# Timing a GpSimd queue of indirect DMAs by ScalarE's probabilities instead of VectorE's maxima

## The chip, the cores and the metric

One NeuronCore of a Trainium2 chip runs the whole kernel. The metric is the device time of one execution in microseconds. The engines are TensorE (PE for matmuls, PEld for weight loads), VectorE (DVE), ScalarE (ACT), GpSimd (POOL) and SyncE (SP); each works through its own instructions in order, and they wait for one another on semaphores.

## The reference, cut to what matters

```python
# x: (B=2, L=2048, D=256); 16 heads of 16, so 32 (batch, head) pairs; TOP = L // 5 = 409
h = _layernorm(x) * (1 + ca) + sa
Q, K, V = proj(Wq, bq), proj(Wk, bk), proj(Wv, bv)            # each (32, 2048, 16)
_, top_idx = jax.lax.top_k(jnp.linalg.norm(Q, axis=2), 409)   # 409 queries per head
Q_sel = take_along_axis(Q, top_idx)
attn = softmax(Q_sel @ K.T * 0.25)                            # (32, 409, 2048)
out_full[top_idx] = attn @ V                                  # the other rows stay zero
x = x + ga * (out_full @ Wo.T + bo)
x = x + gb * moe(_layernorm(x) * (1 + cb) + sb)               # 8 experts, top 2
```

The change concerns the attention of the 409 selected queries over all 2048 keys, head by head. Here a "head" is one of the 32 (batch, head) pairs, counted n = 0 to 31.

## The kernel before, in words

The program is a sequence of blocks: setup, projection, selection of the top queries (`select_block`), attention (`attend_block`, from L797), routing and experts. Only `attend_block` is touched.

Within it, one head goes through five engines, and the work of neighbouring heads is interleaved:

- **SP** loads the keys of head n + 4 into one of four buffers (L869 to L876).
- **POOL** gathers the 409 selected query rows from DRAM by index: three indirect DMAs of 128 rows each (`gather_chunk`, L880 to L882) and, for four heads at once, one of the 25 last rows of each (`gather_tails`, L889). It copies a head's values into a padded layout (`spread_v`, L895). It writes the results back with indirect DMAs of the same kind: three per head (`scatter_chunk`, L899) and one for the tails of four heads (`scatter_tails`, L914).
- **PE** computes each head's scores twice. First as thirteen "chunks" a = 0 to 12 with the queries on partitions (`scores_chunk`, L1086, matmuls at L1094 and L1097), only so that the row maximum can be taken. Then as sixteen "tiles" j = 0 to 15 with the keys on partitions (`scores_tile`, L1101, matmul at L1110). The products with the values are `values` (L1113, matmul at L1120), four groups per head. `results` (L1124) adds up and turns the output; `turn_q` (L1059, L1065, L1069) transposes gathered queries; `turn_max` (L1132) transposes the maxima.
- **DVE** reduces each chunk to a maximum (`maximum`, L960, TENSOR_REDUCE at L963, semaphore `a_done`, thirteen per head), and normalises the results (`finish`, L979 to L988, semaphore `out_done`).
- **ACT** turns each tile into probabilities (`probability`, L1030, ACTIVATE at L1033, semaphore `prob_done`, sixteen per head). It also copies the transposed queries (L1024), the maxima (L1028) and the products (L1038).

The order on PE, ACT and DVE is written out by hand in their `run(n, u)`. In step n PE makes the tiles 0 to 15 of head n; beside tiles 1 to 7 the chunks 6 to 12 of head n + 1; beside tiles 9 to 14 the chunks 0 to 5 of head n + 2. `turn_q(n + 3)` stands at tile 8, `values(n, 0)` at tile 9, `values(n, 1)` at tile 11, `values(n, 2)` after tile 14, `values(n - 1, 3)` at tile 2 and `results(n - 1)` at tile 5. The heads 0 to 3 and 28 to 31 are written out straight; the heads 4 to 27 run in a hardware loop of four heads per trip (`steps`, L851), whose waits take their numbers from registers. POOL's program has no loop: L934 is a Python loop, so all its waits are for constants.

In step n POOL does up to nine things in this order: gathers of head n + 4 (chunks 0, 1, 2), `spread_v(n + 3)`, scatters of head n - 1 (chunks 0, 1, 2), and in every fourth step one tail scatter and one tail gather. Before each of the gathers, each of the scatters and the tails it calls `turn(n, at)` with `at` = 0 to 6, and this waits until another engine has come to a given place. In the kernel before that engine is DVE: `a_done` has to reach 13 (n + 1) + 7, 9, 11, 13, 15, 17, 19. In step n, counted in chunks, this is after the maxima of chunks 6, 8, 10 and 12 of head n + 1 and of chunks 1, 3 and 5 of head n + 2. The `min` in `turn` keeps the number within what DVE ever reaches: in step 31 all seven waits are for the last maximum of all.

Of the kernel before, what the change touches and what calls it, by code (L numbers as in the profile page):

```python
# [29 lines left out]
N = B * H  # L30
TPB = L // P
# [29 lines left out]
def wait(eng, sem, value):  # L61

    if isinstance(value, int) and value <= 0:
        return
    eng.wait_ge(sem, value)
# [731 lines left out]
def attend_block(nc, ctx, io, cst):  # L797

    with ExitStack() as own:
# [4 lines left out]
        NA = FULL * NK + 1  # L804
# [28 lines left out]
        a_ps, a_done, mrow_ps, mrow_done = sem("a_ps"), sem("a_done"), sem("mrow_ps"), sem("mrow_done")  # L833
        b_ps, prob_done, pv_ps, pvs_done, out_ps, out_done = sem("b_ps"), sem("prob_done"), sem("pv_ps"), sem("pvs_done"), sem("out_ps"), sem("out_done")
# [26 lines left out]
        def has(n):  # L861

            return not isinstance(n, int) or 0 <= n < N

        with nc.Block() as block:

            @block.sync
            def _(sp):
                def load_k(n, u):  # L869

                    wait(sp, b_ps, TPB * (n - U + 1))
                    rows = io["k3_d"][bass.ds(n, 1)].rearrange("a r d l -> (a r d) l")
                    for at, count in STACK_K:
                        sp.dma_start(kt[u][at * HD:(at + count) * HD, :], rows[0:count * HD, :]).then_inc(k_here[u], 16)

                steps(sp, load_k)  # L876

            @block.gpsimd
            def _(pool):
                def gather_chunk(n, c):  # L880
                    pool.indirect_dma_start(out=qsel[n % U][:, c, :], out_offset=None, in_=io["q3_d"],  # L881
                                            in_offset=bass.IndirectOffsetOnAxis(ap=cst["idx"][:, n, c:c + 1], axis=0)).then_inc(q_here[n % U], 16)  # L882

                def gather(n):
                    wait(pool, q_ps, n - U + 1)
                    for c in range(FULL):
                        gather_chunk(n, c)

                def gather_tails(g):  # L889

                    wait(pool, q_ps, GH * g)
                    pool.indirect_dma_start(out=qtail[:, :], out_offset=None, in_=io["q3_d"],
                                            in_offset=bass.IndirectOffsetOnAxis(ap=cst["tidx"][:, g:g + 1], axis=0)).then_inc(tail_here, 16)

                def spread_v(n):  # L895
                    wait(pool, pv_ps, GRP * (n - U + 1))
                    pool.tensor_copy(vh[n % U][:, :, 0:HD], vn[:, :, n, :]).then_inc(vh_done, 1)

                def scatter_chunk(n, c):  # L899
                    pool.indirect_dma_start(out=io["attn_d"], out_offset=bass.IndirectOffsetOnAxis(ap=cst["idx"][:, n, c:c + 1], axis=0),  # L900
                                            in_=outs[n % 2][:, c, :], in_offset=None).then_inc(scattered[n % 2], 16)

                def scatter(n):
                    pool.wait_ge(out_done, n + 1)
                    for c in range(FULL):
                        scatter_chunk(n, c)

                TURNS = (7, 9, 11, 13, 15, 17, 19)

                def turn(n, at):  # L910

                    wait(pool, a_done, min(NA * (n + 1) + TURNS[at], NA * N))

                def scatter_tails(g):  # L914

                    pool.wait_ge(out_done, GH * (g + 1))
                    pool.indirect_dma_start(out=io["attn_d"], out_offset=bass.IndirectOffsetOnAxis(ap=cst["tidx"][:, g:g + 1], axis=0),
                                            in_=otail[:, g, :], in_offset=None).then_inc(tail_out, 16)

                gather_tails(0)  # L920
                for n in range(3):
                    gather(n)
                step = Chain(pool, g_step)
                step(pool.memset(fold[:, :], 0.0))
                for g in range(GRP):
                    last = pool.affine_select(out=fold[:, :], in_=fold[:, :], compare_op=ALU.not_equal, fill=1.0,
                                              base=-32 * g, pattern=[[-1, HD + 1]], channel_multiplier=1)
                    if g < GRP - 1:
                        step(last)
                last.then_inc(fold_done, 1)  # L930
                for n in range(3):
                    spread_v(n)
                gather(3)
                for n in range(N):  # L934
                    if has(n + 4):
                        pool.wait_ge(q_ps, n + 1)
                        for c in range(FULL):
                            turn(n, c)
                            gather_chunk(n + 4, c)
                    if has(n + 3):  # L940
                        spread_v(n + 3)
                    if has(n - 1):
                        pool.wait_ge(out_done, n)
                        for c in range(FULL):
                            turn(n, FULL + c)
                            scatter_chunk(n - 1, c)
                    turn(n, 2 * FULL)
                    if n % GH == 1 and n > 1:
                        scatter_tails(n // GH - 1)
                    if n % GH == 0 and n // GH + 1 < GN:  # L950
                        gather_tails(n // GH + 1)
                scatter(N - 1)
                scatter_tails(GN - 1)
                for u in range(2):
                    pool.wait_ge(scattered[u], 16 * FULL * N // 2)
                pool.wait_ge(tail_out, 16 * GN)
# [933 lines left out]
```

## Time and profile before

| | us |
|---|---|
| median of 3 runs | 1300.29 |
| lowest and highest | 1293.09, 1305.63 |
| the profiled execution | 1293.09 |
| its span, first to last instruction | 1291.3 |

The profiled execution is the lowest of the three. In a row of the timeline, the first two numbers are the start and the length in us from the start of the span; `x2` means that so many instructions in a row were merged; in square brackets stand the idle time of the engine just before the row and what ended it.

### The profile page before, as it was taken

How to read it: one execution, taken by the hardware profiler on the slowest of the kernel's cores; microseconds unless marked ns; L12 is line 12 of the kernel's file. 1: busy time of each engine (PE TensorE's matmuls, PEld its weight loads, DVE VectorE, ACT ScalarE, POOL GpSimd, SP SyncE). 2: the span in 40 equal slices, each digit the busy share in tenths (PEclk: the TensorE clock that was granted, in tenths of full speed). 3: DMA queues.
4: the chain of work that ended last, by engine and by line, in shares of the span. 5: the costliest groups of instructions: out<-in, count | busy, mean ns of one | idle time of the engine just before them, and what ended most of it. 6: DMA issues, size and time to landing. Idle time of an engine off the chain costs nothing. (4 is left out here: it accounts for less than half of the span.)

```text
span 1291.3 us, 29412 instructions
## 1 busy us (share of the span) xinstructions
PE 1041.9 (81%) x7670; PEld 644.4 (50%) x7671; DVE 928.4 (72%) x2313; ACT 638.0 (49%) x1387; POOL 637.2 (49%) x660
## 2 busy tenths in 40 slices
PE   7997102699999999999947744599999999999991
PEld 4443002133333333333335631488888888888881
DVE  4884788787777777768438869477777777777771
ACT  2776274276676766667724520244444444444440
POOL 1787380455555455544258950244455444444541
PEclk9999555599999999989969965799999999999996
DMA  6344860111111111111049920122333222222325
GB/s 212 115 155 153 263 209 25 33 44 37 40 43 31 42 32 43 30 43 29 4 143 274 286 89 1 34 39 45 49 49 48 46 44 45 45 49 49 48 35 146
DMA packets 84388, 101.56 MB, mean 79 GB/s; under 512 B 17008, under 2 KB 71984, under 8 KB 84208
## 3 DMA queue, kind: packets, MB, share of 16 engines
q1 hardware_dynamic: 60792, 74.31, 19.0%
q0 software_dynamic: 21632, 23.11, 11.1%
q10 hardware_dynamic: 1912, 3.54, 0.8%
q8 instruction: 22, 0.36, 0.1%
q14 instruction: 30, 0.25, 0.1%
HBM read 62.26 MB, written 42.84 MB: 81 GB/s over the span
## 5 line engine op out<-in xcount | busy, mean ns | idle before, releaser
L963 DVE TENSOR_REDUCE attend_mxh<-attend_p_a 128x1 f32<-128x512 f32 x416 | 265.4, 686 | 83.8 <-PE attend_p_a L1094 64.6
L1033 ACT ACTIVATE w<-attend_p_b 128x409 f32<-128x409 f32 x480 | 227.4, 515 | 119.8 <-PE attend_p_b L1110 92.4
L1755 ACT ACTIVATE expert_hr<-expert_p,b1t 128x256 f32<-128x256 f32 x312 | 131.0, 471 | 223.3 <-PE expert_p L1706 219.7
L1667 POOL DMA_INDIRECT acc_d<-expert_ys,expert_drop x78 | 126.8, 1626 | 209.9 <-DVE expert_ys L1788 182.3
L1720 PE MATMUL expert_p<-w,expert_hhi 128*128 x1248 | 213.7, 273 | 5.8 <-DVE expert_hlo L1813 4.9
L1706 PE MATMUL expert_p<-expert_xhi,w 128*128 128x256 f16 x1248 | 214.3, 274 | 3.6 <-DVE expert_xlo L1796 1.5
L1720 PE MATMUL expert_p<-w,expert_hlo 128*128 x624 | 170.1, 273 | 0.0
L1110 PE MATMUL attend_p_b<-attend_qt,w 98*128 98x409 bf16 x480 | 164.9, 347 | 1.5 <-issue 1.2
L1094 PE MATMUL attend_p_a<-w,attend_qt 96*128 96x512 bf16 x384 | 151.8, 399 | 8.8 <-ACT attend_qt L1024 6.4
L900 POOL DMA_INDIRECT attn_d<-attend_outs,idx x96 | 93.9, 978 | 114.0 <-DVE attend_mxh L963 99.0
L1720 PEld LDWEIGHTS expert_p<-w,expert_hhi 128*128 128x128 f16 x1248 | 121.8, 98 | 28.7 <-issue 11.6
L881 POOL DMA_INDIRECT attend_qsel<-q_d,idx x96 | 92.2, 960 | 88.4 <-DVE attend_mxh L963 69.5
L1706 PEld LDWEIGHTS expert_p<-expert_xhi,w 128*128 x1248 | 122.7, 98 | 23.3 <-issue 8.4
L1659 POOL DMA_INDIRECT expert_xs<-h_d,expert_take x78 | 86.5, 1109 | 84.1 <-DVE expert_take L1792 61.2
L1120 PE MATMUL attend_p_o<-w,attend_vh 128*32 128x409 f32 x1024 | 116.3, 526 | 5.8 <-issue 2.8
L1706 PE MATMUL expert_p<-expert_xlo,w 128*128 128x256 f16 x624 | 119.9, 274 | 0.0
L1811 DVE CAST expert_hhi<-expert_hr 128x512 f16<-128x512 f32 x156 | 67.8, 435 | 65.9 <-ACT expert_hr L1755 64.5
L1813 DVE TENSOR_TENSOR expert_hlo<-expert_hr,expert_hhi 128x512 f16<-128x512 f32 x156 | 109.1, 700 | 5.4
L1110 PEld LDWEIGHTS attend_p_b<-attend_qt,w 98*128 98x128 bf16 x480 | 46.4, 98 | 116.4 <-ACT w L1033 77.1
L1706 PEld LDWEIGHTS expert_p<-expert_xlo,w 128*128 x624 | 61.4, 98 | 7.2
L1720 PEld LDWEIGHTS expert_p<-w,expert_hlo 128*128 128x128 f16 x624 | 61.1, 98 | 6.2
L1747 ACT ACTIVATE expert_xhi<-expert_p_x 128x512 f16<-128x512 f32 x39 | 23.3, 597 | 79.6 <-PE expert_p_x L1692 79.6
(303 smaller groups left out, 1694.6 us busy)
## 6 DMA issues: line engine op xcount, KB each, us to landing
q_d<-project_q SPq DMA_DIRECT2D x32, 256.0 KB
w<-in_L_ffn_w SPq DMA_DIRECT2D x16, 512.0 KB, 3.9
route_wraw<-in_L_ffn_w SPq DMA_DIRECT2D x16, 512.0 KB, 4.9
w<-k_d SPq DMA_DIRECT2D x32, 192.0 KB
k_d<-project_k SPq DMA_DIRECT2D x45, 128.0 KB
x<-in_L_attn_x SPq DMA_DIRECT2D x8, 512.0 KB, 11.2
attn_d<-zero SPq DMA_DIRECT2D x8, 512.0 KB
w<-k_d SPq DMA_DIRECT2D x32, 128.0 KB
```

Of the source, the lines that this page charges most:

```text
L881: pool.indirect_dma_start(out=qsel[n % U][:, c, :], out_offset=None, in_=io["q3_d"], in_offset=bass.IndirectOffsetOnAxis(ap=cst["idx"][:, ...
L900: pool.indirect_dma_start(out=io["attn_d"], out_offset=bass.IndirectOffsetOnAxis(ap=cst["idx"][:, n, c:c + 1], axis=0), in_=outs[n % 2][:, ...
L963: dve.tensor_reduce(mxh[:, c, k:k + 1], chunk_bank(a)[:, :], AX, ALU.max).then_inc(a_done, 1)
L1033: act.activation(prob[:, j, :], tile_bank(j)[:, 0:TOP], ACT.Exp, scale=SCALE).then_inc(prob_done, 1)
L1094: last = pe.matmul(into[:, :], qt[u][0:KR, c * P:(c + 1) * P], kt[u][0:KR, k * CH:(k + 1) * CH], start=True, stop=True)
L1110: pe.matmul(tile_bank(j)[:, 0:TOP], kt[u][0:KR + 2, j * P:(j + 1) * P], qt[u][0:KR + 2, 0:TOP], start=True, stop=True).then_inc(b_ps, 1)
L1120: last = pe.matmul(p_o[32 * w:32 * w + VC, 0:TOP], vh[u][:, j, :], prob[:, j, :], start=(g == 0), stop=(g == TPB // GRP - 1), tile_positio ...
L1667: pool.indirect_dma_start(out=io["acc_d"], out_offset=bass.IndirectOffsetOnAxis(ap=drop[u][:, s:s + 1], axis=0), in_=ys[u][:, s, :], in_of ...
L1706: last = pe.matmul(p_1[g][:, f, :], w, xp[u][:, k, :], start=(n == 0), stop=(n == 3 * KD - 1))
L1720: last = pe.matmul(p_2[s][:, 0:D], hp[u][:, f, s * P:(s + 1) * P], w, start=(f == 0 and n == 0), stop=(f == FB - 1 and n == 2))
L1755: act.activation(hr[g % 2][:, f, :], p_1[g][:, f, :], ACT.Relu, bias=cst["b1t"][:, bass.ds(e * FB + 2 * g + f, 1)], scale=1.0 / WSCALE).th ...
L1813: dve.tensor_tensor(hlo[u][:, 2 * g:2 * g + 2, :], hr[g % 2][:, :, :], hhi[u][:, 2 * g:2 * g + 2, :], ALU.subtract).then_inc(hlo_done, 1)
```

## The change

One table and one wait of the POOL program. The seven turns wait for ACT's probabilities of step n's own head, `prob_done`, sixteen per head, in place of DVE's maxima. The value for turn 0 is 16 n, that is, all tiles of head n - 1; for n = 0 it is zero and `wait` leaves it out. The others are reached after tiles 2, 4, 7, 10, 12 and 14 of head n. Nothing is added or taken away, on any engine; each operation's order on its queue stays.

```diff
-                TURNS = (7, 9, 11, 13, 15, 17, 19)
+                TURNS = (0, 3, 5, 8, 11, 13, 15)
 
                 def turn(n, at):
 
-                    wait(pool, a_done, min(NA * (n + 1) + TURNS[at], NA * N))
+                    wait(pool, prob_done, TPB * n + TURNS[at])
```

The waits beside them stay: `gather` for `q_ps`, `spread_v` for `pv_ps`, the scatters for `out_done`.

## Rows read from the trace of the kernel before

**Rows 1.** Busy time by stage. Columns as in the header line.
```profile
core 0: us, PE busy (x) PEld busy (x) DVE busy (x) ACT busy (x) POOL busy (x), PEclk, DMA share, GB/s
261.27:296.23 34.96, 34.96 (x266) 12.82 (x265) 28.87 (x66) 25.96 (x59) 19.11 (x22) 1.00 0.17 42
296.23:601.97 305.74, 290.86 (x2115) 103.82 (x2112) 232.99 (x528) 205.86 (x458) 161.38 (x180) 0.98 0.15 38
601.97:634.96 32.99, 32.53 (x234) 11.58 (x232) 25.04 (x60) 24.91 (x55) 10.02 (x11) 1.00 0.05 15
```

**Rows 2.** Waits of POOL, 296 to 590 us.
```profile
POOL attn_d L900 <- DVE attend_mxh L963: 67.7, 63, 2.5
POOL attend_qsel L881 <- DVE attend_mxh L963: 51.0, 30, 4.4
```

**Rows 3.** Timeline of ACT: tile 0 (from bank p_a) and tiles 14, 15, straight heads.
```profile
272.90 0.51 ACT L1033 ACTIVATE w<-attend_p_a 128x409 f32<-128x409 f32 x1
...
283.06 0.51 ACT L1033 ACTIVATE w<-attend_p_b 128x409 f32<-128x409 f32 x1
284.12 0.51 ACT L1033 ACTIVATE w<-attend_p_b 128x409 f32<-128x409 f32 x1 [0.55 <-issue]
284.53 0.51 ACT L1033 ACTIVATE w<-attend_p_a 128x409 f32<-128x409 f32 x1
```

**Rows 4.** Timeline of ACT: head 4 and its neighbours.
```profile
296.23 0.51 ACT L1033 ACTIVATE w<-attend_p_a 128x409 f32<-128x409 f32 x1
...
302.19 0.92 ACT L1033 ACTIVATE w<-attend_p_b 128x409 f32<-128x409 f32 x2 [1.06 <-PE attend_p_b L1110]
...
306.66 0.51 ACT L1033 ACTIVATE w<-attend_p_b 128x409 f32<-128x409 f32 x1
308.37 0.51 ACT L1033 ACTIVATE w<-attend_p_b 128x409 f32<-128x409 f32 x1 [1.20 <-PE attend_p_b L1110]
308.78 0.51 ACT L1033 ACTIVATE w<-attend_p_a 128x409 f32<-128x409 f32 x1
```

**Rows 5.** Timeline of POOL: head 4's step.
```profile
297.82 0.99 POOL L881 DMA_INDIRECT attend_qsel<-q_d,idx  x1 [2.27 <-DVE attend_mxh L963]
299.11 0.96 POOL L881 DMA_INDIRECT attend_qsel<-q_d,idx  x1 [0.30 <-issue]
300.38 0.95 POOL L881 DMA_INDIRECT attend_qsel<-q_d,idx  x1 [0.30 <-issue]
301.34 0.41 POOL L897 COPY attend_vh<-v 128x256 f32<-128x256 f32 x1
303.58 1.01 POOL L900 DMA_INDIRECT attn_d<-attend_outs,idx  x1 [1.84 <-DVE attend_mxh L963]
305.56 0.97 POOL L900 DMA_INDIRECT attn_d<-attend_outs,idx  x1 [0.98 <-DVE attend_mxh L963]
306.84 0.96 POOL L900 DMA_INDIRECT attn_d<-attend_outs,idx  x1 [0.30 <-DVE attend_mxh L963]
308.11 0.99 POOL L892 DMA_INDIRECT attend_qtail<-q_d,tidx  x1 [0.30 <-issue]
```

**Rows 6.** Timeline of PE: tile 15 of head 4 and what precedes it.
```profile
306.52 0.90 PE L1120 MATMUL attend_p_o<-w,attend_vh 128*32 128x409 f32 x8
307.34 0.35 PE L1110 MATMUL attend_p_b<-attend_qt,w 98*128 98x409 bf16 x1
```

**Rows 7.** Timeline of DVE: the two maxima before head 4's first gather.
```profile
296.32 1.29 DVE L963 TENSOR_REDUCE attend_mxh<-attend_p_a 128x1 f32<-128x512 f32 x2 [0.90 <-PE attend_p_a L1094]
```

**Rows 8.** Timeline of ACT: head 8.
```profile
346.11 0.51 ACT L1033 ACTIVATE w<-attend_p_a 128x409 f32<-128x409 f32 x1
...
350.71 0.51 ACT L1033 ACTIVATE w<-attend_p_b 128x409 f32<-128x409 f32 x1 [1.65 <-issue]
...
358.66 0.51 ACT L1033 ACTIVATE w<-attend_p_a 128x409 f32<-128x409 f32 x1
```

**Rows 9.** Timeline of POOL: first gather and tail gather of step 8, first gather of step 9.
```profile
347.16 0.98 POOL L881 DMA_INDIRECT attend_qsel<-q_d,idx  x1 [2.22 <-DVE attend_mxh L963]
...
358.01 0.99 POOL L892 DMA_INDIRECT attend_qtail<-q_d,tidx  x1 [0.30 <-issue]
359.83 0.96 POOL L881 DMA_INDIRECT attend_qsel<-q_d,idx  x1 [0.83 <-DVE attend_mxh L963]
```

**Rows 10.** Timeline of ACT: tile 3 of head 9, tile 0 of head 10.
```profile
361.29 0.51 ACT L1033 ACTIVATE w<-attend_p_b 128x409 f32<-128x409 f32 x1 [1.31 <-PE attend_p_b L1110]
...
372.10 0.51 ACT L1033 ACTIVATE w<-attend_p_a 128x409 f32<-128x409 f32 x1 [0.32 <-PE attend_p_b L1110]
```

**Rows 11.** Instructions of two lines: count, then shortest/median/longest in ns.
```profile
L963 DVE TENSOR_REDUCE attend_mxh<-attend_p_a x416: 669/681/693, 235.2 to 630.0; 128x1 f32<-128x512 f32 x139
...
L900 POOL DMA_INDIRECT attn_d<-attend_outs,idx x96: 956/972/1017, 268.0 to 650.3; - x96
```

**Rows 12.** Timeline of POOL: third scatter of step 2, a straight head.
```profile
282.96 0.96 POOL L900 DMA_INDIRECT attn_d<-attend_outs,idx  x1 [0.30 <-DVE attend_mxh L963]
```

**Rows 13.** Timeline of POOL: the end of the block.
```profile
642.52 0.96 POOL L900 DMA_INDIRECT attn_d<-attend_outs,idx  x1 [0.64 <-issue]
647.81 0.96 POOL L900 DMA_INDIRECT attn_d<-attend_outs,idx  x1 [4.33 <-DVE attend_otail L987]
```

## The prediction

> **What bounds the kernel now.** I read the busy times by stage first, then who waits for whom, then the timelines of POOL, ACT and PE side by side for single heads.
>
> The stage that the change touches runs from about 249 to 645 us. The stretches by stage [rows 1] part it in three: heads 1 to 3 (straight), heads 4 to 27 (loop), heads 28 to 30 (straight). In the first PE is busy 34.96 of 34.96 us, 11.65 us a head. In the loop it is busy 290.86 of 305.74 us: 12.74 us a head, 12.12 of them busy. DVE has 232.99, ACT 205.86, POOL 161.38, that is 53% for POOL. So PE sets the pace, in a ring with ACT and DVE, whose results free PE's banks. POOL is not short of time: the waits of POOL [rows 2] show 67.7 + 51.0 us in which it stood in a turn behind a DVE maximum.
>
> So POOL's turns cost nothing directly. What can be had or lost is the difference between a loop head and a straight one, 12.74 - 11.65 = 1.09 us, over 24 heads 26.1 us, 2.0% of the whole. Where is it? Tile 0 of each head marks its start on ACT. A straight head takes 284.53 - 272.90 = 11.63 us, and its tiles 14 and 15 start 1.06 us apart [rows 3]. Head 4 takes 308.78 - 296.23 = 12.55; its tiles 14 and 15 stand 308.37 - 306.66 = 1.71 apart, and ACT had been idle 1.20 us behind PE; it had also been idle 1.06 us before tile 8 [rows 4]. Yet PE's row of tile 15 begins at 307.34 and takes 0.35 [rows 6]: it was finished, by that record, 0.68 us before ACT got it. In that time POOL's third scatter ran, 306.84 to 307.80 [rows 5]. The late tile 8 (302.19) likewise comes after the gathers and the copy, which ended at 301.75 [rows 5]. I read this as PE's completions coming late beside POOL's indirect DMAs. It is an inference from coincidence: in the straight head a third scatter at 282.96 stands just as close to tile 14 (283.06) and delays nothing [rows 3, 12].
>
> **The change part by part.** Nothing is added, so the sum is made of places. How far does each POOL operation move?
>
> - From the maximum to its gather: the maximum of chunk 6 ends at 296.32 + 0.69 = 297.01, the gather starts at 297.82 [rows 5, 7], 0.81 later. A POOL operation behind another follows it by 0.30 [rows 5].
> - Turn 0 now waits for tile 15 of the head before. In head 4's frame that is 0.41 before tile 0 (308.37 against 308.78 [rows 4]) plus 0.51 for the tile: it ends at 0.10. With the 0.81 the first gather starts at 0.9, where it is now at 297.82 - 296.23 = 1.59. It comes 0.7 us earlier.
> - Turns 1 and 2 (tiles 2 and 4) are then met about when POOL is free; the gathers follow at some 2.2 and 3.5, the copy ends near 4.8, now at 5.52: 0.7 earlier.
> - The scatters wait for `out_done` (finish, unchanged) and tiles 7, 10 and 12. They come at roughly 6.5, 7.8 and 9.6, now at 7.35, 9.33 and 10.61 [rows 5]: 0.9 to 1.5 earlier. The tails wait for tile 14 (306.66 - 296.23 = 10.43, plus 0.51) and come near 11.2, now 11.88.
>
> What each is worth:
>
> 1. *Third scatter.* At 9.6 to 10.6 it is over before `values(n, 2)` (306.52, that is 10.29 [rows 6]) is half done. If the scatter is what holds tile 15, the heads without tails (two in four, 12 of the loop) get 1.71 - 1.06 = 0.65 us each: -7.8 us. In the other 12 the tails now stand where the scatter stood, and I count nothing. From below the gain is zero, since in the straight head the coincidence costs nothing.
> 2. *Gathers.* Tile 8 could come earlier, but I count zero. Head 8 is the trial: its first gather starts 347.16 - 346.11 = 1.05 after tile 0, 0.54 earlier than in head 4 [rows 8, 9]. The stall did not go; it moved to tile 6, 1.65 us [rows 8]. The head takes 358.66 - 346.11 = 12.55 us, exactly as head 4. What is cover here is the ring through `results`, `finish` and `values(n, 0)`, which ends at the same place either way.
> 3. *First gather against `values(n - 1, 3)`.* Both are now released by the same event, the end of tile 15. Head 9 shows the bad case: tails of the step before at 358.01, first gather at 359.83, 1.17 after its tile 0 [rows 8, 9], and tile 3 is late by an idle time of 1.31 us; the head takes 372.10 - 358.66 = 13.44 [rows 10], 0.89 more than head 4. Three loop heads (9, 21, 25; the rows are of 9) show it, all directly behind a tail gather. After the change two heads in four stand behind tails with a gather at 0.9. I charge the 9 of these 12 that do not have it now: 9 x 0.89 = +8.0 us. Bounds: 0 (head 8's gather at 1.05 delayed no tile 3) and 21 heads x 0.89 = +18.7.
>
> Free things: step 0 loses its first wait, so one gather is issued earlier, in a prologue where no turn follows it. Steps 30 and 31 are now paced, where most of their waits used to be for the last maximum; their scatters end by 643.48, and the next operation starts at 647.81, behind `out_done`, with 4.33 us idle before it [rows 13]. That is the cover; a delay over 4 us would be needed to reach the end. The key loads on SP wait for `b_ps` and are passed by nothing.
>
> Sum: -7.8 + 0 + 8.0 = +0.2 us. On the profiled execution's own 1293.09 that gives 1293.3. This execution is 0.55% below the median of the runs, so on the scale of the median the forecast is 1300.29 + 0.2, about 1300.
>
> A rule bears on term 3 and on the whole. The maxima's durations are 669 to 693 ns over 416 instructions, and the scatters' 956 to 1017, wherever the two meet [rows 11]: neither slows the other. The Trainium skill (SBUF — State Buffer, on which operations share GpSimd's port) says the same: `tensor_reduce` on trn2 never contends with GpSimd, and a DMA does not contend with a compute engine. By that rule alone the place of an indirect DMA is free, and the sum would be 0, 1300 us; by the late tiles, it is the difference of two terms of 8 us.
>
> **The rivals.**
>
> *Unchanged, the forecast* (chance 0.48): the stalls move and the ring gives the same period, as between heads 4 and 8; about 1300.
>
> *Faster* (0.25): with POOL 0.7 to 1.5 us earlier, gathers, scatters and PE's odd groups no longer meet. For: PE is busy without a gap in the straight heads; 0.65 us per head hang at tile 15. Against: head 8. All of it would be 26.1 us, 1274; half of it, 1287. It decides from 13 us on, 0.54 us a loop head.
>
> *Slower* (0.27): one mechanism, term 3 everywhere. The first gather at 0.9 always starts within `values(n - 1, 3)`, which needs the same tile 15, and tile 3 waits for the gather. 21 heads x 0.89 = 18.7 without the gain of term 1: 1319. Over the four straight heads with a gather too it is 25 x 0.89 = 22.3, 1322. It counts as slower from 15 heads on (15 x 0.89 = 13.3). For: heads 9, 21, 25. Against: head 8, whose gather at 1.05 does nothing to tile 3 [rows 8, 9].
>
> *The turns do nothing at all*, because POOL would be held by `out_done` and its own backlog: then again 1300; it is inside the first case. The idle times of POOL [rows 2] speak against it: it does stand in the turns.
>
> **How the numbers follow.** Likeliest is the unchanged time, 1300. The range leaves out one in ten at either side: below it goes to most of the faster case, 1278; above to the slower one's, 1320. Faster by over 1% (below 1287) takes nearly all of the faster case, slower by over 1% the slower one, and the rest falls within 1%: 0.24, 0.27 and 0.49. 1% is about what a measurement of this kernel tells from no change.
>
> **What would show it.** On POOL's timeline the first gather of a loop step should stand about 0.9 us after tile 0, the third scatter near 9.6, and its releaser should be ACT's L1033. If term 1 holds, tiles 14 and 15 stand 1.06 apart in heads without tails. If term 3 holds, tile 3 has over a microsecond of idle time before it and the tile-to-tile period is near 13.4. If a loop head takes about 12.5 with the stall at tile 6, term 2 is right. I am wrong if the loop falls below 12.2 or rises above 13.3 us a head, or if anything outside 249 to 645 us moves by more than a microsecond or two.

## The result and the profile after

The changed kernel takes 1315.58 us at the median of 13 runs (1309.08 to 1323.44), the kernel before 1305.63 at the median of 13 (1293.09 to 1310.72). The ratio is 1.0083, with a 95% interval of 1.0061 to 1.0105: slower by 0.8%, a little but outside the uncertainty of the measurement.

The profiled execution of the changed kernel took 1324.97 us (span 1323.2), more than any of its 13 timed runs, and the one of before (1293.09) was the fastest of its. The traces therefore show 31.9 us where the medians show 10. I read the kind of the loss from them, not its size, which is about three times too large; the second profile of the same kernel, in the experiments, is nearer to the medians.

Busy time by stage of the changed kernel; the stretches are the same pieces of work as the first two in [rows 1], cut where tile 0 of heads 1, 4 and 28 starts on ACT: the straight heads 1 to 3, and the 24 heads of the loop.

```profile
core 0: us, PE busy (x) PEld busy (x) DVE busy (x) ACT busy (x) POOL busy (x), PEclk, DMA share, GB/s
266.06:300.95 34.89, 34.89 (x266) 12.76 (x265) 28.88 (x66) 25.56 (x58) 18.92 (x22) 1.00 0.18 42
300.95:633.74 332.79, 313.14 (x2114) 107.43 (x2113) 236.28 (x528) 205.22 (x457) 160.81 (x180) 0.90 0.14 35
```

The straight heads 1 to 3 take 34.89 us, before 34.96. The loop takes 332.79 us, before 305.74: 13.87 us a head against 12.74, +27.05 us. Head 0 takes 3.4 us more and starts 1.4 us later, which with -0.1 us for heads 1 to 3 makes the 4.7 us by which the loop starts later. Behind the loop the two are alike (1323.2 - 633.74 = 689.5 us, before 1291.3 - 601.97 = 689.3). So 27.05 of the 31.9 us lie in the loop. The number of interest is PEclk: 0.98 in the loop before, 0.90 now. TensorE stands at one of two levels, 1.0 (2.4 GHz) or 0.5 (1.2 GHz), so the mean of 0.90 is 2 x 0.10 x 332.79 = 67 us at the lower one, before 2 x 0.02 x 305.74 = 12 us. The granted clock's own record has 68.3 and 10.2.

POOL's timeline in a loop head, head 7, whose tile 0 starts at 343.53:

```profile
344.44 0.98 POOL L881 DMA_INDIRECT attend_qsel<-q_d,idx  x1 [2.14 <-ACT w L1033]
345.73 0.96 POOL L881 DMA_INDIRECT attend_qsel<-q_d,idx  x1 [0.30 <-issue]
346.99 0.94 POOL L881 DMA_INDIRECT attend_qsel<-q_d,idx  x1 [0.30 <-issue]
347.94 0.40 POOL L897 COPY attend_vh<-v 128x256 f32<-128x256 f32 x1
350.51 1.01 POOL L900 DMA_INDIRECT attn_d<-attend_outs,idx  x1 [2.17 <-ACT w L1033]
352.13 0.97 POOL L900 DMA_INDIRECT attn_d<-attend_outs,idx  x1 [0.61 <-ACT w L1033]
353.93 0.96 POOL L900 DMA_INDIRECT attn_d<-attend_outs,idx  x1 [0.83 <-ACT w L1033]
```

The gathers start 0.91, 2.20 and 3.46 us after tile 0 and the copy ends at 4.81, as forecast (0.9, 2.2, 3.5, 4.8). The first gather and the scatters are released by ACT's L1033. The scatters come at 6.98, 8.60 and 10.40, half a microsecond or more later than forecast (6.5, 7.8, 9.6), because the tiles that release them are late. ACT in the same head:

```profile
343.53 0.51 ACT L1033 ACTIVATE w<-attend_p_a 128x409 f32<-128x409 f32 x1
...
345.99 0.92 ACT L1033 ACTIVATE w<-attend_p_b 128x409 f32<-128x409 f32 x2
348.80 1.72 ACT L1033 ACTIVATE w<-attend_p_b 128x409 f32<-128x409 f32 x4 [1.89 <-PE attend_p_b L1110]
...
354.88 0.51 ACT L1033 ACTIVATE w<-attend_p_b 128x409 f32<-128x409 f32 x1
355.95 0.51 ACT L1033 ACTIVATE w<-attend_p_b 128x409 f32<-128x409 f32 x1 [0.56 <-PE attend_p_b L1110]
356.49 0.51 ACT L1033 ACTIVATE w<-attend_p_a 128x409 f32<-128x409 f32 x1
```

Tiles 14 and 15 are 1.07 us apart, as in a straight head; in head 4 of before it was 1.71 [rows 4]. Tile 15, preceded by over a microsecond of idle time in 14 of the 24 loop heads before, is so in one now (head 16). In its place tile 6 is late (348.80, idle time 1.89), by over a microsecond in 20 of 24 heads; before it was in 4. PE and DVE at that place:

```profile
346.15 1.00 PE L1129 MATMUL attend_p_o<-attend_fold,attend_pvs 128*128 128x17 f32 x8
347.08 0.35 PE L1110 MATMUL attend_p_b<-attend_qt,w 98*128 98x409 bf16 x1
...
349.36 0.35 PE L1110 MATMUL attend_p_b<-attend_qt,w 98*128 98x409 bf16 x1 [0.53 <-ACT w L1033]
```
```profile
348.83 0.69 DVE L963 TENSOR_REDUCE attend_mxh<-attend_p_a 128x1 f32<-128x512 f32 x1 [1.54 <-PE attend_p_a L1097]
```

By its record PE has tile 6 (347.08) done at 347.43; ACT starts on it 1.37 us later. DVE takes up its next chunk at about the same moment, 348.83. The third gather's issue ended at 347.93. Over the 20 heads ACT takes up the late tile 6 between 0.48 and 0.98 us behind the end of that issue (15 of them 0.83 to 0.98) and never ahead of it. PE itself then stands for 0.53 us, for a bank that ACT has not freed. In the straight heads 1 to 3 of the same trace the third gather stands at the same place, 3.35 to 3.46 us after tile 0, and tile 6 is not late.

What this does to TensorE's clock is seen two heads on. Head 9 starts at 368.96, has the same late tile at 374.27 (ACT idle for 1.94 us), and takes up PE's work again at 374.84:

```profile
368.96:382.94 13.98, 13.28 (x90) 4.52 (x89) 9.91 (x22) 8.52 (x21) 7.12 (x9) 0.88 0.15 35
375.30:378.70 3.40, 3.28 (x13) 0.66 (x12) 3.06 (x11) 1.87 (x5) 1.26 (x2) 0.50 0.01 2
351.87:355.27 3.40, 3.37 (x27) 0.99 (x26) 3.24 (x8) 2.23 (x5) 1.93 (x2) 1.00 0.04 10
```

These are three stretches of the view by stage: head 9; 3.40 us in it from 375.30; and a stretch of equal length at the same place of head 7. In the second PE is at the lower level and starts 13 matmuls where it starts 27 in the third. Tiles 10 and 12 of head 9 are late for that. There are 20 such stretches of 3.4 us in the loop, three before.

The account of the loop's +27.05 us, from the starts of tile 0 and the granted clock of each head:

| loop heads | before | after |
|---|---|---|
| never at the lower level | 22, mean 12.55 us | 9, mean 12.63 us |
| one stretch at it | 1, 14.08 us | 10, mean 13.92 us |
| two | 1, 15.51 us | 5, mean 15.99 us |

With 12.63 as the base, the ten heads cost 10 x 1.29 = 12.9 us, the five 5 x 3.36 = 16.8, together 29.7; the two before cost 4.5 over 12.55; and 24 x 0.08 = 1.9 is left between the bases. 29.7 - 4.5 + 1.9 = 27.1 us. So nearly the whole loss of the trace is in heads in which TensorE's clock fell. Not all of it is the clock's: the table sorts heads, it does not separate causes. Of the 20 stretches 13 lie in 11 of the 20 heads with a late tile 6 (the other nine have none), five in the three heads in which tile 3 was late by about 1.7 us (5, 22, 26) and two in head 16, whose tile 9 was late by 3.47 us. Head 12 is the only one with two stretches and no late tile before them but tile 6, and it takes 15.16 us; the second profile, below, has two more, 15.26 and 15.35 us. By their price two falls cost 2.5 to 2.8 us and not 3.36, and the rest is the late tile 3 or 9 itself: an estimate from three heads.

### The profile page after: what moved, and what is told of

The parts are those of the page before. It is cut to its first block and busy times, and to the rows that moved or that the text cites. A ratio compares the mean times of both kernels' runs of the same rounds, so it can differ in the third digit from the quotient of the medians.

```text
span 1323.2 us, 29411 instructions
## 1 busy us (share of the span) xinstructions
PE 1071.1 (81%) x7670; PEld 650.9 (49%) x7671; DVE 933.8 (71%) x2313; ACT 636.5 (48%) x1387; POOL 632.1 (48%) x660
## 5 line engine op out<-in xcount | busy, mean ns | idle before, releaser
L963 DVE TENSOR_REDUCE attend_mxh<-attend_p_a 128x1 f32<-128x512 f32 x416 | 269.5, 687 | 110.5 <-PE attend_p_a L1094 65.9
L1033 ACT ACTIVATE w<-attend_p_b 128x409 f32<-128x409 f32 x480 | 225.9, 515 | 151.3 <-PE attend_p_b L1110 138.7
L1110 PE MATMUL attend_p_b<-attend_qt,w 98*128 98x409 bf16 x480 | 172.6, 364 | 8.4 <-ACT w L1033 8.4
L1094 PE MATMUL attend_p_a<-w,attend_qt 96*128 96x512 bf16 x384 | 160.8, 422 | 5.9 <-ACT attend_qt L1024 4.7
L1720 PEld LDWEIGHTS expert_p<-w,expert_hhi 128*128 128x128 f16 x1248 | 121.8, 98 | 29.7 <-issue 13.0
L1120 PE MATMUL attend_p_o<-w,attend_vh 128*32 128x409 f32 x1024 | 129.8, 582 | 2.4 <-issue 1.4
L1659 POOL DMA_INDIRECT expert_xs<-h_d,expert_take x78 | 82.7, 1060 | 83.5 <-DVE expert_take L1792 60.6
```

The costliest lines, as they stand in the source:

```text
L963: dve.tensor_reduce(mxh[:, c, k:k + 1], chunk_bank(a)[:, :], AX, ALU.max).then_inc(a_done, 1)
L1033: act.activation(prob[:, j, :], tile_bank(j)[:, 0:TOP], ACT.Exp, scale=SCALE).then_inc(prob_done, 1)
L1094: last = pe.matmul(into[:, :], qt[u][0:KR, c * P:(c + 1) * P], kt[u][0:KR, k * CH:(k + 1) * CH], start=True, stop=True)
L1110: pe.matmul(tile_bank(j)[:, 0:TOP], kt[u][0:KR + 2, j * P:(j + 1) * P], qt[u][0:KR + 2, 0:TOP], start=True, stop=True).then_inc(b_ps, 1)
L1120: last = pe.matmul(p_o[32 * w:32 * w + VC, 0:TOP], vh[u][:, j, :], prob[:, j, :], start=(g == 0), stop=(g == TPB // GRP - 1), tile_positio ...
L1720: last = pe.matmul(p_2[s][:, 0:D], hp[u][:, f, s * P:(s + 1) * P], w, start=(f == 0 and n == 0), stop=(f == FB - 1 and n == 2))
```

## The experiments

The question: is it the new place of the three gathers that makes tile 6 late and lets the clock fall, or the place of the scatters, or a loop on one of the engines, whatever POOL does?

One thing has to be known to read the numbers. The kernel before itself takes about 1302 to 1315 us in some sessions on a chip and about 1267 in others. The same chip was met in both conditions in two cases, so it is neither the chip nor the kernel alone. Each ratio is against the kernel before in the same session.

| | kernel before, median us | runs of this study |
|---|---|---|
| late tiles | 1302 to 1315 | the first result, e5, e10, e13 and e14, e17 |
| no late tile | 1266 to 1269 | e1 to e4, e6 to e9, e11, e12, e15 and e16, e18 |

### The changed kernel again

No edit. What was expected:

> The changed kernel once more, unaltered, beside the kernel before. Experiments 1 to 4 ran on a chip whose loop heads all take 11.6 us with no late tile. Theory E (the loss exists only where TensorE's completions come late; where loop heads take 11.6 us the turns' places cost nothing): if the kernel before takes about 1268 us here, ratio 1.000 within 0.3%; if it takes about 1305 us, ratio near 1.008 with tile 6 late in nearly all loop heads. Theory F (the change costs in itself, by ACT's semaphore or the earlier places): ratio 1.005 or more in either.

Measured: 1315.37 us against 1302.24, ratio 1.0134 [1.0066, 1.0203]. The loop, by stage:

```profile
297.27:621.31 324.04, 309.08 (x2114) 107.35 (x2113) 235.56 (x528) 204.44 (x457) 160.83 (x180) 0.91 0.15 35
```

It takes 13.50 us a head with 2 x 0.09 x 324.04 = 58 us at the lower level, and tile 6 is late in 23 of 24 heads. The reading repeats, at a size nearer to the medians. The other executions bear it out: the mean granted clock of the four of the changed kernel is 0.874 to 0.886, that of the seven of before 0.884 to 0.898. The changed kernel as it stands was timed in sessions with late tiles alone.

### The gathers alone

The three gathers wait for the probabilities, the scatters and tails for the maxima as before.

```diff
-                    wait(pool, a_done, min(NA * (n + 1) + TURNS[at], NA * N))
+                    if at < FULL:
+                        wait(pool, prob_done, TPB * n + PROBS[at])
+                    else:
+                        wait(pool, a_done, min(NA * (n + 1) + TURNS[at], NA * N))
```

> Turns 0 to 2 (the gathers) as after, turns 3 to 6 (scatters, tails) as before. Theory A (the loss comes from the gathers: the second and third stand beside the turned results of the head before, tile 6 is late by some 2.4 us, and TensorE's clock falls to its lower level afterwards): tile 6 late in nearly every loop head, tile 15 late as before as well, half-clock time in the loop 40 us or more, and the time at or above the changed kernel's, ratio to before 1.008 or more. Theory B (the loss comes from the scatters and tails in their new places): ratio within 0.3% of 1.

> As experiment 1, for a chip with late tiles. Theory A (gathers' places cost, scatters' places do not): tile 6 late, half-clock time of 40 us or more, ratio 1.008 or more. Theory B: ratio within 0.3% of 1.

> As experiments 1 and 7, which met chips without late tiles; this one should meet a chip with them, and then decides. If the kernel before takes about 1302 us here: theory A (gathers' places cost, scatters' do not) expects tile 6 late, half-clock time of 40 us or more and ratio 1.008 or more; theory B (the scatters' and tails' places cost) expects a ratio within 0.3% of 1. If the kernel before takes about 1267 us, a ratio of 1.000 under both.

Measured: 1.0002 [0.9985, 1.0019] and 0.9998 [0.9980, 1.0016] in sessions without a late tile, with loop heads of 11.63 us. In a session with late tiles 1351.83 us against 1302.53, ratio 1.0394 [1.0342, 1.0445]. Its loop, and ACT, PE and POOL in head 6, whose tile 0 starts at 331.42 (its line numbers are 4 higher from L907 on):

```profile
301.21:659.58 358.37, 325.71 (x2115) 108.94 (x2113) 236.73 (x528) 207.95 (x458) 160.84 (x180) 0.86 0.14 32
```
```profile
331.42 0.51 ACT L1037 ACTIVATE w<-attend_p_a 128x409 f32<-128x409 f32 x1
331.83 0.91 ACT L1037 ACTIVATE w<-attend_p_b 128x409 f32<-128x409 f32 x2
335.24 0.51 ACT L1037 ACTIVATE w<-attend_p_b 128x409 f32<-128x409 f32 x1 [2.51 <-DMA x<-in_L_attn_x]
```
```profile
332.57 0.35 PE L1114 MATMUL attend_p_b<-attend_qt,w 98*128 98x409 bf16 x1
...
336.21 1.00 PE L1133 MATMUL attend_p_o<-attend_fold,attend_pvs 128*128 128x17 f32 x8 [2.29 <-ACT attend_pvs L1042]
```
```profile
332.18 0.98 POOL L881 DMA_INDIRECT attend_qsel<-q_d,idx  x1 [0.46 <-issue]
333.47 0.96 POOL L881 DMA_INDIRECT attend_qsel<-q_d,idx  x1 [0.30 <-issue]
```

The loop takes 14.93 us a head with 2 x 0.14 x 358.37 = 100 us at the lower level. PE has tile 3 (332.57) done at 332.92 by its record; ACT starts on it at 335.24, 2.32 us later and 0.81 behind the end of the second gather (334.43). The releaser that the row names, a load of `x`, was over long before; the wait in the code is for PE. PE stands for 2.29 us. Tile 3 is late in 11 heads, tile 6 in 12 and tile 15, as before the change, in 7. So the gathers alone do more harm than the whole change: the two halves do not add up. One late tile lies outside the loop, in head 1, where every engine's program is straight: PE's record of tile 6 ends at 269.55, ACT starts on it at 270.79, 1.24 us later and 0.85 behind the end of the third gather (269.94).

### The scatters alone

The same edit with `at >= FULL`.

> Turns 0 to 2 as before, turns 3 to 6 as after. Theory A: tile 15 on time, tile 6 late in few heads; each head without a tail gains up to 0.65 us, ratio 0.993 to 1.000, and no more half-clock time than before (about 10 us). Theory B: slower, ratio 1.005 or more.

> As experiment 2, for a chip with late tiles. Theory A: tile 15 on time (1.06 us after tile 14) in heads without tails, half-clock time no more than before, ratio 0.993 to 1.000. Theory B (the scatters' places cost): ratio 1.005 or more.

> Scatters and tails by ACT, gathers by DVE, alone in its session. Experiment 10 met late tiles and took 1351.8 us against 1302.5, on the very chip where experiment 1, the same kernel, had none; so late tiles are a condition of the session and not of the chip. If the kernel before takes about 1302 us here, theory A expects tile 15 on time in heads without tails, half-clock time no more than before, ratio 0.985 to 1.000; theory B (scatters' places cost too) a ratio of 1.005 or more.

> Scatters and tails by ACT, gathers by DVE. Counts only in a session with late tiles (kernel before near 1302 us). Theory A (the gathers' new places alone do the harm): tile 15 on time in heads without tails, half-clock time no more than before, ratio 0.985 to 1.000. Theory B: ratio 1.005 or more.

Measured: 0.9996 [0.9978, 1.0014], 0.9990 [0.9971, 1.0009] and 0.9983 [0.9969, 0.9998] without late tiles. With them 1311.56 us against 1315.0, ratio 0.9988 [0.9963, 1.0013]. The loop, and ACT and POOL in head 6 (tile 0 at 332.93):

```profile
304.88:622.68 317.80, 290.69 (x2114) 103.95 (x2113) 233.06 (x528) 207.05 (x457) 160.83 (x180) 0.99 0.15 36
```
```profile
336.74 1.04 ACT L1037 ACTIVATE w<-attend_p_b 128x409 f32<-128x409 f32 x2 [0.56 <-issue]
339.61 0.51 ACT L1037 ACTIVATE w<-attend_p_b 128x409 f32<-128x409 f32 x1 [1.82 <-PE attend_p_b L1114]
```
```profile
336.99 0.94 POOL L881 DMA_INDIRECT attend_qsel<-q_d,idx  x1 [0.30 <-issue]
337.94 0.40 POOL L897 COPY attend_vh<-v 128x256 f32<-128x256 f32 x1
338.72 1.00 POOL L900 DMA_INDIRECT attn_d<-attend_outs,idx  x1 [0.37 <-issue]
```

Tile 6 (336.74) is on time and so is tile 15, except in head 16. In its place tile 8 waits for 1.82 us, in 23 of 24 heads; the first scatter follows the copy now without a turn between. A head takes 13.24 us, more than in the trace of before (12.74), but with only 6.8 us at the lower level of the clock. The two traces are of different sessions; against its own session's runs of before nothing is gained or lost. So a late tile alone does not lower the clock: among the 23 heads with a late tile 8, by 1.79 to 2.50 us, one has a fall (head 5), and the other fall is in head 16. Taking away tile 15's stall brought nothing.

Here the granted clock and the time do not go together. Over its ten executions the clock was 0.897 to 0.903, over the 19 of before 0.884 to 0.894. From clock and span of each, the medians lie some 31 us apart in time at the lower level, an estimate; the time is 3.4 us less. What the clock gave back went to the stalls at tile 8.

The straight heads matter most here. Heads 1 to 3, in which no engine is in a loop yet, take 12.96, 13.05 and 13.02 us, and in each tile 9 is late. ACT, PE and POOL in head 1 (tile 0 at 265.85):

```profile
273.33 0.51 ACT L1037 ACTIVATE w<-attend_p_b 128x409 f32<-128x409 f32 x1 [2.03 <-PE attend_p_b L1114]
```
```profile
271.08 0.35 PE L1114 MATMUL attend_p_b<-attend_qt,w 98*128 98x409 bf16 x1
```
```profile
271.56 1.01 POOL L900 DMA_INDIRECT attn_d<-attend_outs,idx  x1 [0.26 <-issue]
```

PE's record of tile 9 ends at 271.43, ACT starts on it 1.90 us later, 0.76 behind the end of the first scatter (272.57). It is the same picture as in the loop, with waits for constants on all engines.

### TensorE's program without its loop

The 32 steps of PE written out one after another, so that its waits are for constants; in the kernel before (e3) and in the changed one.

```diff
-                steps(pe, run)
+                for n in range(N):
+                    run(n, n % U)
```

> The kernel before, but TensorE's program of the attention written out straight for all 32 heads, so that its waits have constants; ACT, DVE and SP keep their loop. Theory C (completions of TensorE come late only where its own program is in the loop, as the straight heads suggest): all heads near 11.65 us, 22 to 27 us less in the loop, ratio near 0.98. Theory D (it is POOL's DMAs alone, or the loop of ACT and DVE): heads stay at 12.5 to 12.7 us, ratio within 0.5% of 1.

> The changed kernel with TensorE's program written out straight. Theory C: heads near 11.65 us and the same time as its counterpart with the old turns within 0.3%, so that the change costs nothing there. Theory D: tile 6 stays late, clock falls stay, 10 us slower than its counterpart.

> As experiment 4, for a chip with late tiles: the changed kernel with TensorE's program straight. Theory C (late completions need TensorE's loop): all heads near 11.65 us, ratio to before 0.975 to 0.985. Theory H (they need POOL's DMAs and a chip of this kind, not the loop): tile 6 late as with the loop, ratio 1.008 or more.

> The changed kernel with TensorE's attention program straight, alone in its session. If the kernel before takes about 1302 us here: theory C (late completions need TensorE's loop) expects all heads near 11.65 us and a ratio of 0.97 to 0.98; theory H (they need POOL's DMAs in such a session, not TensorE's loop) expects tile 6 late and a ratio of 1.008 or more.

> The changed kernel with TensorE's attention program straight. Counts only in a session with late tiles. Theory C (late completions need TensorE's loop): heads near 11.65 us, ratio 0.97 to 0.98. Theory H (they need POOL's DMAs in such a session, not the loop): tile 6 late, ratio 1.008 or more.

Measured without late tiles: e3 1.0011 [0.9993, 1.0029], e4 1.0015 [0.9996, 1.0035], e9 0.9986 [0.9969, 1.0003], e12 0.9994 [0.9978, 1.0011]. With them (e14): 1314.34 us against 1315.0, ratio 1.0006 [0.9978, 1.0035]. Its loop, and ACT at tile 6 of head 8 (tile 0 at 351.76):

```profile
299.42:619.38 319.96, 304.73 (x2114) 106.67 (x2113) 235.62 (x528) 204.92 (x458) 160.84 (x180) 0.93 0.16 37
```
```profile
356.88 1.32 ACT L1033 ACTIVATE w<-attend_p_b 128x409 f32<-128x409 f32 x3 [1.87 <-PE attend_p_b L1110]
```

Tile 6 is late in 23 of 24 heads, by 1.1 to 2.0 us, and 2 x 0.07 x 319.96 = 45 us are at the lower level. PE's loop is not what makes the tiles late. Yet the ratio is neither the 0.97 to 0.98 of theory C nor the 1.008 or more of theory H: beside these runs of before the new turns with a straight TensorE cost nothing against the kernel before, although their granted clock was lower (0.879 to 0.887, before 0.884 to 0.894). Either the straight program takes off what the turns cost, or the turns cost less there; the changed kernel itself was not timed beside them. A head without a fall takes 12.37 us, against 12.63 and 12.53 in the two traces of the changed kernel (heads other than 16), but these are different sessions. The kernel before with a straight TensorE (e3) met no session with late tiles.

The traces without late tiles show what the same places of POOL do when nothing is late. In e4, head 8 (tile 0 at 342.31), with the loops of ACT and DVE and all of POOL's new turns:

```profile
346.11 0.92 ACT L1033 ACTIVATE w<-attend_p_b 128x409 f32<-128x409 f32 x2 [0.56 <-PE attend_p_b L1110]
...
353.81 0.51 ACT L1033 ACTIVATE w<-attend_p_a 128x409 f32<-128x409 f32 x1
```
```profile
345.64 0.94 POOL L881 DMA_INDIRECT attend_qsel<-q_d,idx  x1 [0.30 <-ACT w L1033]
```

The third gather stands 3.33 us after tile 0, as in head 8 of the changed kernel's trace, and ACT takes up tile 6 in the midst of it, 346.11. The head takes 11.50 us, the 24 of them 11.63 on average, at full clock. In such a session I see nothing to lose or win by POOL's places.

### No gathers at all

The changed kernel with POOL's three gathers of each step, those of heads 4 to 31, left out together with their turns; PE's wait for them is made a constant, and the attention of these heads works on the queries of heads 0 to 3 instead, the 25 last rows apart. So the kernel leaves out part of the computation.

> The changed kernel without the three gathers of each step (turns 0 to 2 go with them): the heads from 4 on compute with the queries of heads 0 to 3, so that part of the computation is left out; copies, scatters, tails and everything on the other engines stay. On a chip with late tiles: theory A (the gathers beside results and tile 6 make tile 6 late, and the falls of TensorE's clock follow from that) expects no late tile 6, no half-clock time in the loop, and loop heads of 11.7 to 12.0 us against 13.5 with gathers. Theory G (the late tiles come from TensorE's loop or the chip itself, whatever POOL does) expects 12.4 us and more, with tile 6 late.

> As experiment 6: the changed kernel without the gathers of heads 4 to 31 (these heads compute with the queries of heads 0 to 3; that part is left out). Counts in a session with late tiles. Theory A (the gathers make tile 6 late and bring the clock falls): no late tile 6, little or no half-clock time in the loop, loop heads of 11.7 to 12.3 us. Theory G (the late tiles do not hang on POOL's DMAs): tile 6 late, 12.4 us and more.

> The changed kernel with no gathers in heads 4 to 27 (POOL's three are left out, the attention of heads 4 to 27 takes the queries of heads 0 to 3), a third time, since both runs before met a session in which no tile comes late. If the kernel before again takes over 1300 us on this chip: theory A (the gathers at their new place make tile 6 late, and TensorE's clock falls behind it) expects no late tile 6, under 10 us at half clock in the loop and loop heads of 12.0 to 13.1 us; the rival (ACT's and DVE's loops are late by themselves, whatever POOL issues) expects tile 6 late as before, 45 to 60 us at half clock and heads of 13.3 to 13.9 us. If the kernel before takes under 1270 us here, the run tells only that the loop head is 11.63 us once more.

Measured: 1274.32, 1274.89 and 1271.62 us against 1265.89, 1267.52 and 1265.71, ratios 1.0062 [1.0042, 1.0082], 1.0050 [1.0027, 1.0074] and 1.0042 [1.0029, 1.0056]. All three met sessions without late tiles, and their loop heads take 11.63 us as everyone's there. In e6, e16 and e18 some 6 to 7 us more than in e1 and e4 stand behind the attention, in blocks that get other data; I have not followed them up. The runs do not say whether a late tile needs a gather: that stays open.

### All three programs without loops

`steps` itself written out, so that PE, ACT, DVE and SP wait for constants throughout; the changed kernel otherwise, with every one of POOL's operations.

```diff
-            for c in range(U):
-                run(c, c)
-            with eng.Fori(1, N // U - 1) as i:
-                for c in range(U):
-                    run(U * i + c, c)
-            for c in range(U):
-                run(N - U + c, c)
+            for n in range(N):
+                run(n, n % U)
```

> The changed kernel with the attention programs of all engines straight: no hardware loop, every wait for a constant. Counts in a session with late tiles. Theory J (the late tiles need the loops of ACT and DVE, whose waits take their numbers from registers; TensorE's loop is not needed, as experiment 14 showed): heads 4 to 27 near 11.65 us, ratio to before 0.96 to 0.975. Theory H (POOL's DMAs in such a session are enough): tile 6 late, ratio 1.00 or more.

> As experiment 15, for a session with late tiles (kernel before at 1300 us or more). Theory J (the late tiles need the loops of ACT and DVE): heads 4 to 27 near 11.65 us, ratio 0.96 to 0.975. Theory H (POOL's DMAs in such a session are enough): tile 6 late, ratio 1.00 or more.

Measured: without late tiles 1269.23 us against 1267.52, ratio 1.0007 [0.9989, 1.0025]. In a session in which the kernel before took 1302.93 us: 1272.87, ratio 0.9776 [0.9734, 0.9818], a little above the 0.96 to 0.975 expected. What had been its loop, and ACT, PE and POOL in head 8 (its line numbers are 5 lower):

```profile
296.16:578.99 282.83, 280.85 (x2114) 102.36 (x2113) 231.60 (x528) 206.26 (x457) 161.33 (x180) 0.99 0.18 42
```
```profile
342.68 0.51 ACT L1028 ACTIVATE w<-attend_p_a 128x409 f32<-128x409 f32 x1
...
346.61 1.03 ACT L1028 ACTIVATE w<-attend_p_b 128x409 f32<-128x409 f32 x2 [0.56 <-PE attend_p_b L1105]
...
354.31 0.51 ACT L1028 ACTIVATE w<-attend_p_a 128x409 f32<-128x409 f32 x1
```
```profile
346.23 0.35 PE L1105 MATMUL attend_p_b<-attend_qt,w 98*128 98x409 bf16 x1
```
```profile
346.15 0.95 POOL L876 DMA_INDIRECT attend_qsel<-q_d,idx  x1 [0.30 <-issue]
```

The third gather starts 3.47 us after tile 0, as in head 7 of the changed kernel. PE's tile 6 ends at 346.58 and ACT starts on it at 346.61, while the gather's issue still runs to 347.10; in the changed kernel it took 1.37 us and the end of the gather. The head takes 354.31 - 342.68 = 11.63 us, as do 22 of the 24 (heads 16 and 17 take 12.93 and 14.04, with late tiles of their own, taken up 1.80 and 0.98 us behind PE's records; head 16 has a late tile 9 in all seven traces with late tiles). So without loops the late tiles are gone from 22 heads at these places of POOL. That is not the same as "no loop, no late tile": the straight heads of e10 and e13 have them, and so have heads 16 and 17 here. This version beats the kernel before by 2.2% in such a session and costs nothing in the others.

One rival can be read from the traces: that the engines were late because they waited for their own code. In the loop of the changed kernel the queues of kind "instruction" moved 10 packets, for 24 heads that all had a late tile; in the same heads of the version without loops they moved 32, and two heads had one. The loading of code does not go with the late tiles.

## Why the prediction was wrong where it was

- *The time and the sign.* 1300 was forecast with 1278 to 1320, and 1315.58 lies in the range; that is luck, as the slow end of the range was made of late tiles 3 in 21 to 25 heads, which did not come. The likeliest case, no change, failed: the ratio's interval excludes it. Of the 15.6 us between, 5.3 are the median of before, which stands at 1305.63 over 13 runs where it was 1300.29 over three. By the prediction's own bound it was wrong as well: "above 13.3 us a head" was the limit, and the traces show 13.87 and 13.50.
- *Where POOL's operations go.* Right for the gathers and the copy to 0.1 us. Wrong by 0.5 to 0.8 us for the scatters, since they were placed as if tiles 7 to 12 would keep their times.
- *Term 1, -7.8 us.* Its mechanism held: tile 15 came on time, in the changed kernel and with the scatters alone, and in heads with tails too. Its price did not: the scatters alone gave 0.9988 [0.9963, 1.0013], where -7.8 us would be 0.994. The time went to tile 8, now late by 1.82 us. The prediction had this rule in term 2 (a stall goes, the next one takes its place) and did not apply it to term 1.
- *Term 2, 0 us.* The step that failed. That the head takes "exactly as head 4" is true of a head in which only the tile is late: 12.63 us against 12.55. What the sum lacked is what can follow a tile 6 late by up to 1.9 us: in 11 of the 20 heads with it TensorE's clock fell, and a head with one fall took 1.29 us more. (In four more heads it fell behind a late tile 3 or 9.) The trace of before had the price of a fall, in its heads 21 and 25 (14.08 and 15.51 us), but I priced heads 9, 21 and 25 all by the rows of head 9, the one of them without a fall. It did not show falls behind a late tile 6: its four heads with one had none. I looked at the ring's period and never at the granted clock by head.
- *Term 3, +8.0 us.* Right in kind, wrong in number and price. Tile 3 was late in 6 loop heads of the changed kernel, not in 12. Where it was, the heads took 13.75 to 16.12 us, and not 13.44. With the gathers alone it was late in 11, and such heads took 13.1 to 18.1 us. All but one of them had two or three stretches at the lower level; how the time divides between the clock and the late tile was not measured.
- *The rule on contention.* The maxima last 687 ns on average (669 to 693 in [rows 11]) and POOL's indirect DMAs 0.94 to 1.01 us as before. The Trainium skill's rule (SBUF — State Buffer, on which operations share GpSimd's port) that `tensor_reduce` never contends with GpSimd on trn2 agrees with these durations. The conclusion that I drew from it alone, that the place of an indirect DMA is free, holds in the sessions without late tiles (nine ratios of 0.998 to 1.002 with moved turns) and fails with the gathers alone in a session with them (1.0394): what comes late there is no operation but the moment at which an engine takes up work that, by PE's record, is already done.
- *The rivals.* "Faster" (1274 if the loop heads took 11.65 us) is what the version without loops shows, 1272.87, but POOL's places did not bring it. "Slower" came true in sign, at about half of its 19 to 22 us, by another mechanism for the most part.

*Shown:* the loss of the traces lies in heads in which the clock fell; the gathers' place alone is enough for harm (+3.9%, in one session with four executions); PE's loop is not needed for the late tiles; without all loops they are gone from 22 of 24 heads, in a session in which the kernel before had them. *Argued only:* that POOL's issue of a DMA is what delays an engine's wake-up; it rests on the late tile's following the end of an issue by 0.5 to 1 us, and the kernel without gathers never met the condition. That the fall of the clock, and not the stall before it, makes the head longer by 1.29 us is argued too: no run held the one fixed and changed the other. *Not so:* that a late tile needs a loop; heads 1 to 3 of the scatters alone and head 1 of the gathers alone have none. *Open:* why the loops made most of the heads late where the straight heads with POOL at the same place were not, which of the loops of ACT, DVE and SP matters, whether it is the loop or its waits on registers, and what makes a session one or the other kind. Removing the loops one at a time was not tried except for PE.

## What to carry to other kernels

Price a stall twice: once as idle time in the ring, and once by what the granted clock does behind it. Sort the heads (or trips) of a loop by their period and read the clock of the longest before settling that "the stall only moves". And compare a loop's trips with the same work written out straight: the 1.09 us a head between the two was, here, in sessions with late tiles, a larger prize than this reordering of POOL's queue. Time both kernels in one session, and name the session's level: what costs 3.9% in one cost nothing in another.

## What the runs showed of the hardware

- ACT took up finished work late beside POOL's indirect DMAs: in two loop heads 1.37 and 2.32 us behind the end of PE's record, and DVE started at the same moment as ACT (348.83 and 348.80). In two straight heads, with waits for constants, it was 1.24 and 1.90 us. In the program without loops, with POOL at the places of the changed kernel, it was 0.03 us in head 8.
- This occurs in some sessions and not in others on the same chip: the same kernel, 1267 or 1302 us.
- In the changed kernel's loop TensorE's clock stood at its lower level in 20 stretches of 3.4 us, 13 of them behind a stall at tile 6 (in 11 of 20 such heads). With stalls of 1.79 to 2.50 us at tile 8, in the scatters alone, one of 23 heads had such a stretch. A head with one was 1.29 us longer in the changed kernel's trace.
